# Attention and experts in float32 on one core: the values of four score units stand together, and more units take their maxima from rows

## What is computed

```python
h = relu(conv(emb_table[x]))                     # (2, 1024, 128)
n = layernorm(h)
q, k, v = (proj(n, W) for W in (Wq, Wk, Wv))     # 8 heads of 64
attn = softmax(q @ k.T * 64 ** -0.5)             # 1024 x 1024 for each head and batch
h = h + (attn @ v) @ Wo.T + n
h = h + experts(layernorm(h))                    # fc1, gelu, fc2, next_w, gelu
```

## Time and profile before

| | |
|---|---|
| median of 3 runs | 390.14 us (390.11 to 390.15) |
| profiled execution | 390.13 us |
| its span, first to last instruction | 388.3 us |
| PE, DVE, ACT, POOL busy | 98%, 70%, 71%, 76% |
| mean granted TensorE clock | 0.998 |

### The profile page before, as it was taken

One profiled execution on the slowest core, in us unless ns is written; L12 is line 12 of the kernel. 1 busy time (PEld: TensorE's weight loads), 2 busy tenths in 40 slices (PEclk: granted clock), 3 DMA queues, 4 the chain that ended last, 5 costly groups with the idle time before them and its releaser, 6 DMA issues.

```text
span 388.3 us, 6736 instructions
## 1 busy us (share of the span) xinstructions
PE 378.8 (98%) x2372; PEld 221.9 (57%) x2372; DVE 272.2 (70%) x481; ACT 276.6 (71%) x395; POOL 294.0 (76%) x145
## 2 busy tenths in 40 slices
PE   8999999999999999999999999999999999999996
PEld 7756545544555445445544544454456644589995
DVE  6998677788778787777777777877774545565222
ACT  3566656568878886987788687969885689337753
POOL 3080476949999999999999999999999699700021
PEclk9999999999999999999999999999999999999999
DMA  4001002101132030103010720261052105000001
GB/s 134 20 0 30 24 3 55 56 0 56 22 92 56 3 107 5 54 3 109 3 55 5 216 56 1 56 164 57 4 152 69 54 1 165 0 2 15 14 29 55
DMA packets 28229, 19.46 MB, mean 50 GB/s; under 512 B 21248, under 2 KB 23680, under 8 KB 28196
## 3 DMA queue, kind: packets, MB, share of 16 engines
q1 hardware_dynamic: 27620, 18.05, 17.6%
q10 hardware_dynamic: 576, 0.98, 0.8%
HBM read 17.72 MB, written 1.17 MB: 49 GB/s over the span
## 4 chain that ended last, share of the span: by engine, by line
PE 93%; DVE 4%; issue 1%; ACT 1%; DVEq 0%
PE psum L690 31%; PE psum L679 24%; PE psum L617 11%; PE psum L605 5%; PE psum L626 4%; PE psum L747 4%; PE psum L736 4%; PE psum L581 3%; PE psum L701 2%; PE psum L556 1%; PE psum L642 1%; PE psum L644 1%; PE psum L755 1%; PE psum L530 1%; PE psum L714 1%
## 5 line engine op out<-in xcount | busy, mean ns | idle before, releaser
L1109 DVE TENSOR_REDUCE half_maxes<-psum 128x1 f32<-128x512 f32 x232 | 149.0, 684 | 26.6 <-PE psum L617 25.1
L876 ACT ACTIVATE probs<-psum 128x1024 f32<-128x1024 f32 x128 | 124.7, 1022 | 55.5 <-PE psum L679 55.1
L690 PE MATMUL psum<-probs,v_all 128*64 128x512 f32 x512 | 123.7, 605 | 0.0
L1326 POOL TENSOR_TENSOR sums<-sums,probs 128x1024 f32<-128x1024 f32 x31 | 74.3, 2395 | 3.4 <-ACT probs L876 3.4
L1326 POOL TENSOR_TENSOR odd_sum<-odd_sum,probs 128x1024 f32<-128x1024 f32 x31 | 74.3, 2397 | 0.0
L690 PEld LDWEIGHTS psum<-probs,v_all 128*64 128x64 f32 x512 | 31.3, 136 | 62.2 <-issue 41.9
L1154 DVE TENSOR_SCALAR psum<-max_plane 128x512 f32<-128x512 f32 (+1 forms) x55 | 43.0, 790 | 31.7 <-ACT probs L876 31.7
L1326 POOL TENSOR_TENSOR sums<-probs 128x1024 f32<-128x1024 f32 x16 | 38.0, 2376 | 28.6 <-ACT probs L876 28.1
L617 PE MATMUL psum<-k_round,q_round 64*128 64x512 f32 x256 | 57.3, 448 | 2.3 <-DVE half_maxes L1109 1.4
L617 PEld LDWEIGHTS psum<-k_round,q_round 64*128 64x128 f32 x256 | 24.1, 184 | 54.8 <-DVE half_maxes L1109 42.5
L679 PE MATMUL psum<-q_round,k_round 64*128 64x512 f32 x256 | 52.4, 405 | 0.1
(11 more groups left out here) (123 smaller groups left out, 448.8 us busy)
## 6 DMA issues: line engine op xcount, KB each, us to landing
max_plane<-rows_scratch SPq DMA_DIRECT2D x16, 512.0 KB, 3.7
inv_sb<-inv_scratch SPq DMA_DIRECT2D x14, 256.0 KB, 5.2
max_rows_of<-maxes SPq DMA_DIRECT2D x128, 0.5 KB, 2.0
v_all<-in_fc SPq DMA_DIRECT2D x4, 512.0 KB, 7.7
fc_late<-in_fc SPq DMA_DIRECT2D x4, 512.0 KB, 5.6
out_h<-probs SPq DMA_DIRECT2D x8, 128.0 KB, 1.8
v_all<-in_w ACTq DMA_DIRECT2D x3, 256.0 KB, 3.6
woT<-in_wo SPq DMA_DIRECT2D x1, 256.0 KB, 3.5
```

Source lines behind the costliest of these rows:

```text
L690: last = pe.matmul(out_bank[head_rows(h), :], v_all[:, s, kc, head_rows(h)], probs[unit(s, kc, half) % TILES][:, h, :], start=(kc == 0), s ...
L876: last = act.activation(probs[u % TILES][:, heads, :], source, ACT.Exp, scale=SCALE)
L1109: dve.reduce_max(half_maxes[:, h, qc, keys:keys + 1], slot[:, h, :], AX.X).then_inc(maxed, 1)
L1326: pool.tensor_tensor(chain[:, :, :], first[:, :, :], probs[kc][:, :, :], ALU.add).then_inc(own, 1)
```

## The change

The order of a middle part becomes max, first unit, max, second unit. Value items stand in even turns alone, those of the two turns before together; in step 7 from part 1 on each part has those of the part before, as it was. In steps 0 to 6 the units (4,0), (5,0), (0,1), (1,1), (4,1) and (5,1), given as (kc, half), take their maxima from rows, with the one exception (0,4,0). The order of parts with three max items is the same, except for their values.

```diff
-UNFILLED = BEHIND_Q + BEFORE_K + FIRST_PLANES + [(STEPS - 1, kc, 0) for kc in (4, 5, 6, 7)]
+BEHIND_SCORES = [(s, kc, half) for s in range(STEPS - 1) for kc, half in ((4, 0), (5, 0), (0, 1), (1, 1), (4, 1), (5, 1)) if (s, kc, half) != (0, 4, 0)]
+UNFILLED = BEHIND_Q + BEFORE_K + FIRST_PLANES + BEHIND_SCORES + [(STEPS - 1, kc, 0) for kc in (4, 5, 6, 7)]
...
     else:
-        items = maxes[:1] + [first] + shares[0] + [second] + shares[1] + maxes[1:]
+        items = maxes[:1] + [first] + shares[0] + maxes[1:] + [second] + shares[1]
     items += beside_values(s, part)
     items += [("fill", *u) for u in following if u in SCALAR_FILLED]
-    if turn > 0:
-        items += [("pv", *u) for u in units_of(*divmod(turn - 1, PARTS))]
+    weighed = (turn - 2, turn - 1) if turn % 2 == 0 else ()
+    if s == STEPS - 1 and part > 0:
+        weighed = (turn - 1,)
+    items += [("pv", *u) for t in weighed if t >= 0 for u in units_of(*divmod(t, PARTS))]
```

## The result

The changed kernel takes 434.74 us (median of 4 runs, 434.24 to 435.10) against 390.14: a ratio of 1.114, 95% interval 1.1125 to 1.1158. I had forecast 431.0, in a range of 416 to 441. The profiled execution took 434.24 us with a span of 432.4, so it is 44.1 us longer than the one of before.

What follows compares the result with a forecast made beforehand. PE, busy 98% of the span with back-to-back work, was taken to set the time. Terms 15.1 + 6.0 + 12.3 + 5.1 + 2.5 = 41.0 us on 390.13 gave 431.1, said as 431, range 416 to 441.

Steps and rivals of the forecast that it cites:

- PE's own work grows: On PE: 38 units by rows add 8.7 us, fewer value blocks save 4.8, so 3.9 us more without any wait.
- a round trip: Entering and leaving a block of values on PE: 0.08 us to enter plus 0.20 to leave, 0.28 together.
- The estimate of 0.11: Skill-based price of entering and leaving a value block, 0.11 us instead of 0.28; time would be 2.6 us above the sum.
- The max items lose their cover: In middle steps each max item waits for the previous one's first reduction: gaps 1.31, then 1.38 us.
- inner duo: Parts 1 and 2, or 5 and 6, of a step: 9.11 us against 7.85, twelve times, +15.1 us.
- one with denominators: Parts 3 and 4 taken together: 9.82 us against 8.81, +1.0 six times, +6.0 us.
- The fill behind k: Part 7 and the next part 0: a unit waits 1.8 us for ACT's fill; 13.90 against 11.45, five times, +12.3 us.
- S: Start of k in part 7; the next unit was to wait for its fill until S + 5.22 us.
- My own sign: Forecast counted as wrong if PE's clock showed anything but 9s in the profile after.
- rival 3: PE's clock falls to 1.2 GHz in the 18 pairs of each run: up to 116 us on top, some 545; 2%.
- ACT, POOL, SP, the eight buffers: Middle steps: ACT holds nothing up, POOL gets slack, SP's DMAs stay the same, eight probability buffers still do.
- Rival 1: Reductions don't bind; only PE's work and the waits for fills count: 407 us; 6%.

Runs made afterwards that it cites:

- the last experiment: The changed kernel with reductions over 128 of 512 columns and with parts 7 and 0 having their own values: 396.28 us, ratio 1.016.
- The order alone: The kernel before with only the order max, unit, max, unit, and values in every part as before: 411.48 us, ratio 1.055.
- the short reductions: Reductions inside the steps cut to 128 of 512 columns: 415.25 us in the changed kernel, 386.86 us in the kernel before.

## Why the prediction was right, point by point

- **PE's own work grows.** Right. 38 units cost 8.5 us (8.7 said). The switches saved come out of the last experiment: 0.28 us a round trip, as said. How I had divided it was off: a block of sixteen, its entry included, takes 3.58 us, 0.16 less than two blocks of eight, where I took 0.08 and then put 0.08 in front of the 3.58 as well; by that my duos were 0.08 too long. The estimate of 0.11 that was worked out from the Trainium skill (TensorEngine Tiling, Tiling Modes, with TensorE: Matmul & The Clock Gate, Part 2) would make that duo 8.43 us, and the measured 8.26 is against it.
- **The max items lose their cover.** Right in mechanism and size: 1.30 and 1.38 us to the second and the third (the fourth waits for nothing, 1.42), 9.07 us an inner duo for 9.11 said, 1.0 more for one with denominators. It was read from parts of step 0 that had the new order of items already. The order alone and the short reductions each show it by itself.
- **The fill behind k.** The place, the size (13.75 for 13.90) and the unit's wait until S + 5.1 were right. One wait was missed: the first max item after k and q is the first of that very step, so it waits for ACT's rounding of q (the line `pe.wait_ge(rounded, 2 * v + 2)`), 1.19 us. It cost nothing more, because it runs out before the fill does; but it splits PE's idle time in two and hides the cause from a reader who looks for one wait of 1.8 us.
- **The clock.** Here a step failed: "I hold this unlikely", 2%, for a fall in all runs of units, and "the trace disagrees so far". The stretch that I took as witness had gaps of 0.2 us; the gaps of 1.2 and 1.6 us were new in the middle steps, and behind three of these six places it did fall, for 1.6 us each: 4.8 of the 44.1 us. My own sign, a clock of anything but 9s, came true. It is far from the 545 us of rival 3, and it is what the forecast of 431.1 lacks; without it the profiled execution would have been at 429.4, 1.7 below the forecast: the terms that I did have came to 39.0 us for 41.0 (the 0.35 ahead of the change left out). What the Trainium skill (TensorE: Matmul & The Clock Gate, A second HAM failure mode) says of short idles was the better guide in kind. For the gaps of 0.2 us in the inner duos the trace does not bear it out: no fall in any of them.
- **ACT, POOL, SP, the eight buffers.** Right: none of them appears as a releaser of PE in an inner duo. ACT's exponentials were nearer than "holds nothing up" sounds: 0.7 us of slack in my reckoning, and they bind as soon as the reductions are short.
- **Rival 1** (reductions don't bind, 407) is what the short reductions build; they gave 415.25, with five falls of the clock in it; less 1.6 us for each that is 407.

## What to carry to other kernels

Work that looks like a nuisance between two others may be the cover of a loop between two engines. Before it is joined or moved, write down for each waiting item the loop that it closes (here matmul, reduction, release: 1.38 us) and the work that stands over it in the new order; the profile often holds a stretch, in a prologue or a last step, in which the new order already runs. And a gap on TensorE of a microsecond can have two prices, the gap and what the clock does after it.

## What the runs showed that I had not expected

- The clock fell to 0.50 behind two of five borders whose gaps were 1.2 and 0.4 us, and behind a gap of 1.6 us before step 7, in one execution (mean clock 0.988). The other three executions have a lower mean clock (0.982); where it fell in them isn't on record. Five matmuls whose result nobody reads took the time from 434.74 to 431.11 us.
- A unit filled by rows costs PE 0.23 us in one order and saves 0.3 us net in another: +8.5 us for all 38 in the kernel before, -12.0 us in the new arrangement, because it takes instructions off the queues of ACT and DVE at the moment when these stand between PE and its next bank.
- Three edits that cost 8.5, 21.3 and 45.4 us when made alone cost 44.6 us together. The parts of a change do not add up when each of them moves the same wait.
